# Home-table scatters moved from the first self attention to the first cross-attention, one expert offset read per tile, and earlier loads, in a nine-phase transformer kernel on Trainium2

## The reference, cut to what matters

```python
x = gated_memory(x, ctx)          # softmax over 16 memories, sigmoid gate, rms norm
x = expert_layer(x, ctx, mask)    # layer 1
x = latent_layer(x, media)        # 16 heads of 64, then a gelu feed-forward of 1024
x = expert_layer(x, ctx, mask)    # layer 3

def expert_layer(x, ctx, tt):
    vm = expert_mask(tt)[..., None]                  # which expert each token has
    h = rms_norm(x, ln_in_w)
    q, k, v = split(where(vm, h @ v_qkv, h @ l_qkv)) # 16 heads of 16
    q, k = apply_rotary(q, k, positions)
    a = causal_attention(q, k, v)
    x = x + where(vm, a @ v_dense, a @ l_dense)
    c = attention(rms_norm(x, ln_post_cross_w) @ cq_w, ctx @ ckv_w)
    x = x + c @ cdense_w
    m = rms_norm(x, ln_post_attn_w)
    return x + where(vm, silu(m @ v_gate) * (m @ v_up) @ v_down,
                         silu(m @ l_gate) * (m @ l_up) @ l_down)
```

## Time and profile before

| what | value |
|---|---|
| runs | 2355.1, 2352.7, 2341.13 us; median 2352.7 |
| profiled execution | 2359.21 us; its span in the trace 2357.4 us |
| busy share of the span | PE 90%, DVE 59%, ACT 48%, POOL 35% |
| self attention of layer 1, of layer 3 | 376.6 us, 311.8 us |
| cross-attention of layer 1, of layer 3 | 174.7 us, 173.3 us |

### The profile page before, as it was taken

How to read it: one execution, slowest core, us unless ns; L and a number is a source line. 1 busy time by engine, 2 the same in 40 slices (tenths; PEclk the granted TensorE clock), 3 DMA queues, 4 the chain that set the end, 5 groups by cost and what they waited for, 6 DMA issues and landing times.

```text
span 2357.4 us, 63607 instructions
## 1 busy us (share of the span) xinstructions
PE 2121.8 (90%) x23904; PEld 1692.2 (72%) x23905; DVE 1392.3 (59%) x2863; ACT 1123.1 (48%) x2563; POOL 819.0 (35%) x1045
## 2 busy tenths in 40 slices
PE   8966888878997999699999987997899969979998
PEld 5644666655666999588888877996677746658997
DVE  6753666665774333466666656552788857763333
ACT  4753545436664333344443434444566537763332
POOL 1644545415652222111111111222444426652222
PEclk9977999988997999899999998999999989989999
DMA  7427777722003111300000001002444420011111
GB/s 227 127 68 102 113 109 109 105 45 83 27 29 105 58 58 53 112 2 3 2 3 2 2 2 47 26 20 80 139 130 130 127 89 20 29 42 52 59 59 36
DMA packets 105989, 155.11 MB, mean 66 GB/s; under 512 B 24099, under 2 KB 82288, under 8 KB 105616
## 3 DMA queue, kind: packets, MB, share of 16 engines
q0 software_dynamic: 16560, 55.23, 11.8%
q1 hardware_dynamic: 76288, 78.80, 11.4%
q10 hardware_dynamic: 12896, 17.64, 2.3%
HBM read 86.69 MB, written 56.28 MB: 61 GB/s over the span
## 4 chain that ended last, share of the span: by engine, by line
PE 75%; DVE 6%; DMA 4%; issue 3%; ACT 3%; ACTq 1%; another core or an unknown queue 1%; POOL 0%; SPq 0%; POOLq 0%; DVEq 0%
PE ps_all L2367 3%; PE ps_all L2365 3%; PE ps_all L2366 3%; DMA s_x_in<-x_sorted 3%; PE ps_all L1619 3%; PE ps_all L1591 3%; PE ps_all L1167 2%; PE ps_all L1181 2%; PE ps_all L1199 2%; PE ps_all L1122 2%; PE ps_all L2390 2%; PE ps_all L2392 2%; PE ps_all L2391 2%; PE ps_all L2375 2%; PE ps_all L1605 2%
## 5 line engine op out<-in xcount | busy, mean ns | idle before, releaser
L403 POOL TENSOR_TENSOR a_probs<-a_probs,a_sm 128x1024 f32<-128x1024 f32 x32 | 60.9, 1904 | 351.8 <-DVE a_sm L398 351.8
L1742 POOL TENSOR_TENSOR c_kx<-c_qkt,const 128x512 f32<-128x512 f32 x128 | 130.7, 1039 | 111.3 <-ACT c_qkt L1685 108.2
L1356 POOL TENSOR_TENSOR pool_w<-s_qkt,const 128x512 f32<-128x512 f32 x128 | 132.2, 1056 | 92.9 <-ACT s_qkt L1290 92.2
L2365 PE MATMUL ps_all<-f_wh,f_xh 128*128 x396 | 154.2, 389 | 4.9 <-DVE f_xl L2513 4.9
L2366 PE MATMUL ps_all<-f_wh,f_xl 128*128 x396 | 148.5, 375 | 0.0
L2367 PE MATMUL ps_all<-f_wl,f_xh 128*128 x396 | 148.3, 375 | 0.0
L2508 DVE SCALAR_TENSOR_TENSOR f_h<-ps_all,rstd,f_act_g 128x688 f32<-128x688 f32 x66 | 61.7, 934 | 142.0 <-PE ps_all L2367 128.8
L2086 ACT ACTIVATE self_w<-ps_all,a_q_bias 128x256 f32<-128x256 f32 x128 | 53.7, 471 | 189.5 <-PE ps_all L1930 189.5
L1122 PE MATMUL ps_all<-s_wh,s_xh 128*128 x264 | 102.3, 388 | 27.0 <-issue 15.4
L2390 PE MATMUL ps_all<-f_dh,f_hh 128*128 x396 | 116.9, 295 | 4.0 <-DVE f_hl L2523 4.0
L2429 ACT ACTIVATE f_act_g<-ps_all,rstd 128x688 f32<-128x688 f32 x66 | 55.2, 837 | 131.6 <-PE ps_all L2367 131.6
(11 more groups left out here) (338 smaller groups left out, 6981.9 us busy)
## 6 DMA issues: line engine op xcount, KB each, us to landing
qkv_sorted<-pool_w SPq DMA_DIRECT2D x66, 392.0 KB
pool_w<-pool_w SPq DMA_DIRECT2D x128, 68.0 KB
s_x_in<-x_sorted SPq DMA_DIRECT2D x66, 128.0 KB
f_x_in<-x_sorted SPq DMA_DIRECT2D x66, 128.0 KB, 2.0
x_res<-x_sorted SPq DMA_DIRECT2D x66, 128.0 KB, 2.1
x_sorted<-x_res POOLq DMA_DIRECT2D x1, 4224.0 KB, 17.4
l_rows<-in_x SPq DMA_DIRECT2D x32, 128.0 KB
x_res<-in_x SPq DMA_DIRECT2D x32, 128.0 KB
```

The costliest lines, as they stand in the source:

```text
L1356: ins = nc.gpsimd.tensor_tensor(kx[:, p % 2, c], qkt[:, p % 2, 2 + c].rearrange("p (b k) -> p b k", b=2).unsqueeze(2) .broadcast_to([P, 2, ...
L1742: ins = nc.gpsimd.tensor_tensor(kx[:, p % 2, b], qkt[:, p % 2, 1, b * S:b * S + S].unsqueeze(1).broadcast_to([P, RH, S]), const[:, C_H8X:C ...
L2365: nc.tensor.matmul(bank, x_high, wh[:, w_at], start=(c == 0), stop=False)
```

## The change

1. Gated memory: POOL scatters two pairs per step for one step longer (p = 23 too), so that two scatters are left behind the loop instead of three.
2. Self attention, SP: the load of tile t+3 is issued before `put(t)`, no longer after it.
3. Self attention, PE: the expert's offset is read once per tile, behind the transpose of that tile, and handed to both projections; for tile 0 it is read before the wait for the weights.
4. Self attention, POOL: the gathers of pairs 0 to 2 are issued a tile earlier each, and `put_home` is gone.
5. Cross-attention of layer 1, POOL: `put_home` comes twice per step in steps 0 to 15, ahead of `spread`.
6. Latent attention: the second bank of `k_copy` goes from DVE to ACT, between the two halves of `out_high`; the semaphore for key copies is split in two.

```diff
-                        if 14 <= p < 23:
+                        if 14 <= p < 24:
                             put_sorted(2 * p - 28)
                             put_sorted(2 * p - 27)
-                        if 23 <= p:
-                            put_sorted(p - 5)
-                    for p in range(PAIRS - 3, PAIRS):
+                        if 24 <= p:
+                            put_sorted(p - 4)
+                    for p in range(PAIRS - 2, PAIRS):
                         put_sorted(p)
...
                     for t in range(NT + 4):
+                        if is_tile(t + X_SLOTS):
+                            load(t + X_SLOTS)
                         if is_tile(t):
                             put(t)
-                        if is_tile(t + X_SLOTS):
-                            load(t + X_SLOTS)
                         if has(t - 4):
                             swap(t - 4)
...
-                    def project(t, out, lo, cols):
-                        at = nc.tensor.value_load(off_qkv[0:1, t:t + 1], min_val=0, max_val=CH * 3 * D)
+                    def expert_at(t):
+                        return nc.tensor.value_load(off_qkv[0:1, t:t + 1], min_val=0, max_val=CH * 3 * D)
+
+                    def project(at, t, out, lo, cols):
...
                     x_t(0)
+                    at = expert_at(0)
                     pe.wait_ge(wlow_ok.handle, wlow_ok.at(2 * CH))
                     for t in range(TILES):
-                        proj_qk(t)
+                        proj_qk(t, at)
                         x_t(t + 1)
-                        proj_v(t)
+                        next_at = expert_at(t + 1)
+                        proj_v(t, at)
+                        at = next_at
...
                     for t in range(TILES):
                         rstd_(t + 2)
-                        if has(t - 3):
-                            gather(t - 3)
-                        if n == 1 and has(t):
-                            put_home(t)
+                        if 0 <= t - 2 < 3:
+                            gather(t - 2)
...
-                        if n == 1 and has(p + TILES):
-                            put_home(p + TILES)
                         if has(p + 2):
                             spread(p + 2)
...
                     for p in range(PAIRS + 3):
+                        if n == 1 and has(2 * p):
+                            put_home(2 * p)
+                            put_home(2 * p + 1)
                         if has(p + 2):
                             spread(p + 2)
...
                         if has(p - 1):
-                            out_high(p - 1)
+                            out_high(p - 1, (0,))
+                        if more:
+                            k_copy(g + 1, 2 * i + 1)
+                        if has(p - 1):
+                            out_high(p - 1, (1,))
...
                             softmax_sum(dve, sm, probs, p, p % 2)
-                        if more:
-                            k_copy(g + 1, 2 * i + 1)
                         if has(p - 1):
                             out_low(p - 1)
```

More of the change, by code:

```diff
@@ L226, in build @@
         sel_ok = count("sel_ok")
-        q2_pe, q2_ok, k2_pe, k2_ok, v2_pe = (
-            count(name, 2) for name in ("q2_pe", "q2_ok", "k2_pe", "k2_ok", "v2_pe"))
+        q2_pe, q2_ok, k2_pe, v2_pe = (count(name, 2) for name in ("q2_pe", "q2_ok", "k2_pe", "v2_pe"))
+        k_even_ok, k_odd_ok = count("k_even_ok"), count("k_odd_ok")
         v_half = count("v_half")
@@ L280, in has_group2, with k_units @@
             return g < PAIRS // 2
-        def k_units(p, b):
-            return 4 * (p // 2 + 1) + 2 * (p % 2) + b + 1
+        def k_units(p):
+            return 2 * (p // 2 + 1) + p % 2 + 1
         def steps(eng, step):
@@ L1125, in project, with proj_qk @@
                         return ins
-                    def proj_qk(t):
+                    def proj_qk(t, at):
                         pe.wait_ge(xlow_ok.handle, xlow_ok.at(t + 1))
@@ L1131, in proj_qk, with proj_v @@
                             pe.wait_ge(evac_ok.handle, evac_ok.at(t))
-                        project(t, ps_a[:], 0, 2 * D).then_inc(qk_pe.handle, 1)
-                    def proj_v(t):
+                        project(at, t, ps_a[:], 0, 2 * D).then_inc(qk_pe.handle, 1)
+                    def proj_v(t, at):
                         if v_ok.due(t):
@@ L1763, in put_sorted, with put_home @@
                                                 x_tile(p), None).then_inc(sorted_put.handle, 16)
+                    def put_home(p):
+                        pool.indirect_dma_start(home_d, bass.IndirectOffsetOnAxis(slot_i[:, p:p + 1], 0),
+                                                token_i[:, p:p + 1], None).then_inc(home_put.handle, 16)
                     spread(0)
@@ L1961, in scores @@
                             pe.wait_ge(q2_ok.handle, q2_ok.at(0, 4 * g + 4))
-                            pe.wait_ge(k2_ok.handle, k2_ok.at(0, 4 * g + 4))
+                            pe.wait_ge(k_even_ok.handle, k_even_ok.at(2 * g + 2))
+                            pe.wait_ge(k_odd_ok.handle, k_odd_ok.at(2 * g + 2))
                         if sub_ok.due(p):
@@ L2094, in v_copy, with k_copy, out_high @@
                         nc.scalar.activation(vb[p % 2][0][:], ps_a[:], ACT.Copy).then_inc(v_half.handle, 1)
-                    def out_high(p):
-                        for r, bank in enumerate((ps_o, ps_p)):
+                    def k_copy(g, u):
+                        act.wait_ge(k2_pe.handle, k2_pe.at(0, 4 * g + (u + 1)))
+                        if s_pe.due(2 * g - 2):
+                            act.wait_ge(s_pe.handle, s_pe.at(2 * g - 2))
+                        nc.scalar.activation(kt[:, g % 2, 2 * u:2 * u + 2].rearrange("p j n -> p (j n)"), banks[1], ACT.Copy) \
+                            .then_inc(k_odd_ok.handle, 1)
+                    def out_high(p, halves):
+                        for r in halves:
+                            bank = (ps_o, ps_p)[r]
                             act.wait_ge(pv_pe.handle, pv_pe.at(p, r + 1))
@@ L2115, in _ @@
                     x_high(1)
+                    k_copy(0, 1)
+                    k_copy(0, 3)
                     c_high(1)
@@ L2232, in _ @@
                     x_low(1)
-                    for u in range(4):
-                        k_copy(0, u)
+                    k_copy(0, 0)
+                    k_copy(0, 2)
                     c_low(1)
```

15 lines of the change are left out of this document (6 added, 9 removed).

## The result

The changed kernel took 2295.4 us (median of 4 runs, 2292.57 to 2298.99), against 2352.4 us for the kernel before: a ratio of 0.9768, 95% interval 0.974 to 0.9796. The forecast was 2287 us in a range from 2266 to 2320. The profiled span went from 2357.4 to 2297.2 us, 60.2 us shorter; the forecast was 65.6.

What follows compares the result with a forecast made beforehand. PE was taken to bound most of the span, with holes mainly in layer 1's self attention. Terms -64.8 - 8 - 1.3 + 11 - 2.5 = -65.6 gave 2293.6, less 6.5 to the median: 2287 us, range 2266 to 2320.

Steps and rivals of the forecast that it cites:

- Layer 1's self attention, -64.8 and -4: Homes leaving and the earlier load bring the phase to layer 3's length, -64.8 us; one offset read per tile, -4 us.
- Offset reads, -8: Prologues of both self attentions: reading the offset once shortens PE's 0.90 us holes by 0.72, -4 us per phase.
- Gated memory's tail, -1.3: Behind the gated memory's loop: one scatter fewer saves 0.96 us plus 0.30 us between two, -1.3 us.
- Homes in the cross-attention, +11: Layer 1's cross-attention: two home scatters make POOL's step 6.3 us, 1.2 more than PE's, costing 11 us after slack.
- the transfers' trouble moves along: Rival: home scatters hold up something small in the cross-attention, such as instruction fetches, 15 us, giving 2302 us; chance 0.05.
- the sign that I had named for it: Layer 1's cross-attention: PE idle before the scores, released by POOL's spread in steps 5 to 16, none after.
- Second key bank, -2.5: Latent attention: ACT copying the second bank lets DVE's low part end 0.17 us earlier in 15 even steps, -2.5 us.
- Layer 3's self attention, -4: Layer 3's prologue: one offset read per tile removes 0.72 us from five holes of PE, about -4 us.
- something other than the homes slows layer 1's self attention: Rival: colder weights or instruction fetches, for instance, slow layer 1's transfers, giving 2319 or 2304 us; chance 0.18.
- POOL blocks on the queue: Rival: the queue fills in the cross-attention and home scatters wait to issue, giving 2353 to 2439 us; chance 0.04.
- the homes are free in the cross-attention: Rival: POOL's issue overlaps or the spread has more slack, so +11 falls away, giving 2276 us; chance 0.10.
- the longest issues: Upper bound of the cross-attention term: every home scatter issue taking 1.40 us, cost put at 22 us.

Runs made afterwards that it cites:

- wide_before: Kernel before, with only the home scatters widened to 512 bytes per row, still in layer 1's self attention: 2292.9 us, ratio 0.974.
- wide_self: Changed kernel with home scatters of 512 bytes a row put back in layer 1's self attention, one per tile: 2279.0 us, ratio 0.9699.
- homes_self: Changed kernel with the four-byte home scatters put back in layer 1's self attention, one per tile, out of the cross-attention: 2320.6 us, ratio 0.9842.
- load_after: Changed kernel with the load of tile t+3 again issued behind the write of tile t: 2296.6 us, ratio 0.9763.
- wide_cross: Changed kernel with home scatters of 512 bytes per row in place of 4, same number and places in the cross-attention: 2288.5 us, ratio 0.9727.
- latent_undone: Changed kernel with both key banks of the latent attention copied by DVE again: 2298.5 us, ratio 0.9796.
- no_homes: Changed kernel without any home scatter, the tokens' own numbers standing in the table instead: 2278.0 us, ratio 0.968.
- one_per_step: Changed kernel with one four-byte-row home scatter per step in steps 0 to 31 of the cross-attention, not two in 0 to 15: 2292.8 us, ratio 0.9736.
- wide64_before: Kernel before, with only the home scatters changed to rows of 64 bytes, still in layer 1's self attention: 2294.3 us, ratio 0.9761.
- wide_one: Changed kernel with home scatters of 512 bytes a row, one per step in steps 0 to 31 of the cross-attention: 2277.9 us, ratio 0.9673.

## Why the prediction was right, and where it was off

The sum came within 5.4 us of the profiles' difference, and a part of that is luck: the cross-attention cost 6.6 us more than booked, and the latent attention gave 4.3 us more.

**Layer 1's self attention, -64.8 and -4.** It fell by 68.5 us, and the sum had 68.8. The cause was the one named. With the small home writes gone in any way, moved or widened, the phase takes 306 to 312 us; with them there it takes 355 to 375. The reading of the queue rows was right as to who does it. It was incomplete as to how: it is not that there are scatters on the queue but that their rows are 4 bytes, since as many wide ones in the same place cost nothing that can be measured (wide_before, wide_self). And the gathers and loads were not all that stood: 16.0 us on that phase's chain were waits for the unknown queue. I had also argued that the earlier load alone would not help while gathers are slow. It took ACT's wait for the load from 50.1 to 5.3 us with the scatters in place (homes_self). What I had not seen is how much the earlier load is worth while the scatters are there (part of the 19.4 us) and how little once they are gone (1.6 us in the phase). The two parts overlap, so their gains can't be added.

**Offset reads, -8.** By the profiles 8.0 us, by the medians 8.5. The hole shrank from 0.90 to 0.23 us, by 0.67 where I had 0.72. Right.

**Gated memory's tail, -1.3.** It gave about half. Layer 1's first projection starts 0.8 us earlier, but the hole before it, which is the offset read, fell from 1.09 to 0.23 us, so by all of that. The last scatter's transfer in the chain of waits, before, then changed:

```profile
153.92 2.63 DMA x_sorted<-x_res,slot_i
```
```profile
153.56 3.15 DMA x_sorted<-x_res,slot_i
```

One scatter fewer saved POOL its 1.26 us, but then the last one took longer to land: 3.13 to 3.56 us in the eleven kernels with two scatters behind the loop, 2.56 to 2.63 in the three with three. From the first of these scatters to the last one's landing it is 6.7 us before and 5.9 to 6.4 us in the eleven. The step had the issue and left out the landing. Where that stretch begins varies by more than its gain between the kernels, 149.8 to 151.7 us.

**Homes in the cross-attention, +11.** This step failed in its mechanism and in its size. As a term on POOL it was near: with wide rows it costs 10.2 us. That it came so near is partly luck. At the measured step of 6.1 us the working gives 13 x 1.0 - 5 = 8 us of holes; there were 6.0, and 4.2 us of slower products, which it did not have. But I let POOL's time be the whole price, and held the other path, "the transfers' trouble moves along", for a rival with a chance of 0.05 and 15 us. It happened: +17.6 us in the profile, in which ACT and DVE stood still for 18.3 us on the chain and 22.0 us in all. POOL's lateness was hidden behind those stalls: the sign that I had named for it, PE waiting for the spread before the scores, came to 1.0 us. The two prices overlap: 10.2 for POOL alone and 16.1 for the stalls alone gave 11.0 to 20.8 together, in the four kernels that have both. Where the stalls were short (load_after: 10.0 us, phase 190.1), the phase is as long as with POOL's term alone (189.3). The trace of before had shown it. The waits for a remote queue, 33.2 us in layer 1's self attention and none in layer 3's, are waits of ACT and DVE. I counted them as part of the phase's excess, which goes, and did not ask whether they go with the scatters to the new place. My argument that nothing waits for a transfer in the cross-attention left out the queues that bring instructions.

The Trainium skill's "small, variable" for descriptor generation ("DMA: Bandwidth & Descriptors", "Anatomy of one DMA — SWDGE (gpsimd) path") would have made POOL's part free. The trace disagrees: each scatter held POOL for 0.96 us and 0.30 us before it, and two of them per step made the phase POOL-bound in wide_cross.

**Second key bank, -2.5.** It gave 3 to 7 us: 6.8 between the two profiles, 5.5 in the phase when undone, 3.1 in the medians. This term was undersized because I looked at one waiter only. The groups of the latent attention in the changed kernel (window 951:1323; busy, mean ns, idle before and its releaser):

```profile
L2015 PEld LDWEIGHTS ps_all<-a_oh,a_oth 128*128 128x128 f32 x224 | 42.9, 191 | 12.8 <-DVE a_otl L2227 12.8
...
L1960 PEld LDWEIGHTS ps_all<-pool_w,ctx_all 128*64 128x64 f32 x224 | 13.5, 135 | 20.0 <-ACT a_kt L2107 15.7
```

The dense product's wait fell from 14.9 to 12.8 us, about the 0.1 to 0.2 us per even step that I had worked out. The value projection's wait for the copied bank fell from 22.1 (DVE's copy, 29 pairs) to 15.7 us (ACT's, 28 pairs), and that I had not read. With the copies undone it is 22.1 us again (latent_undone).

**Layer 3's self attention, -4.** It gave 3.4 us.

**The rivals.** That something other than the homes slows layer 1's self attention is ruled out by wide_before, in which only the form of their table changed. That POOL blocks on the queue did not happen: the issue stayed at 0.96 us. That the homes are free in the cross-attention is wrong by 17 to 21 us. Two sums of the working were off. With the longest issues the POOL term would be 13 x 1.92 - 5 = 20 us, not 22. And with 9.3 us per two homes the blocked step would be 3.6 + 9.3 = 12.9 us, not 15.6, which makes 2396 us, not 2439. Neither bears on the forecast.

**What stays open.** That the remote waits are instruction fetches is argued from the share of the instruction queues. It is higher in the phase that has them and back to 0.7 or 0.8% (q8) where the rows are wide. But it does not follow them in size: in the cross-attention q8 has 1.1% with 22.0 us of such waits and 1.2% with 10.0 (load_after). No experiment fed ACT or DVE from elsewhere. Why four-byte writes hold up reads was not shown, only that rows of 64 bytes are enough to end it. Whether it is the bytes that a write carries or the 4 bytes between neighbouring rows of the table stays open too. A run with 4-byte writes to rows 64 bytes apart would tell. Sizes between 4 and 64 were not tried.

## What to carry to other kernels

When two phases with the same code differ, compare their queue rows and their waits for an unknown queue: work that slows everything around it shows there and not in its own row. Before you move such work, ask what it does to its neighbours, and whether a change of its form (here a table with rows of 64 bytes or more in place of 4) removes the cost where it stands. When a term of the sum is a stall that another thing causes, move the stall with the thing that causes it.

## What the runs showed of the hardware

- 32 scatters of 128 four-byte words into a DRAM table with rows of four bytes cost a phase with gathers 43 to 48 us (homes_self against no_homes), and one with few transfers 15 to 16 us beside what they cost on POOL (one_per_step). With rows of 64 or 512 bytes, written whole, and the same number of packets the cost was not measurable (wide_before, wide64_before, wide_one, wide_self).
- "DMA: Bandwidth & Descriptors" of the Trainium skill, in "Specifications", says that transfers under 512 bytes make a DMA engine read, modify and write. A penalty for small writes is in line with these runs, but here it was gone at 64 bytes: 2294.3 us against 2292.9 with 512. That an engine reads before it writes is shown by no run here.
- The penalty fell on others: on gathers on the same queue (7.8 us to landing in homes_self, 4.1 in the changed kernel), and on ACT and DVE in holes of up to 5.5 us. The scatters themselves looked cheap (0.96 us on POOL, 3.6 us to landing in the cross-attention).
- A widening from 4 to 512 bytes a row left POOL's issue at 0.96 us.
